# Decoder layer with expert routing: output products of the second attention as three f32r products

## The chip, the cores and the metric

The kernel runs on 1 core of one Trainium2 chip. The metric is the device time of one execution in microseconds; the median of the runs counts. The engines are named as in the profile: PE is TensorE (PEld its weight loads), ACT ScalarE, DVE VectorE, POOL GpSimd, SP SyncE, which only issues DMAs here.

## What is computed

`x` is 32 sequences of 64 tokens of width 256, `ctx_512` 32 x 64 x 64. Three residual parts follow each other:

```python
x = x + attn(layernorm(x), ...)            # 16 heads of 16, rotary, per-head layernorm, softmax
x = x + xattn(layernorm(x), ctx_512, ...)  # below
x = x + ffn(layernorm(x), ...)             # 8 experts, each token to its best 2, weighted

# xattn: 16 heads, keys and values are the context itself (64 wide, rotated: kv_r)
q_hk = (hidden_q @ Wq.T).reshape(B, S, H, K)
q_big = rope(einsum('bshk,hkq->bshq', q_hk, w_kc_q))
q_r = einsum('bshq,hqr->bhsr', q_big, W_qr)
k_r = einsum('bld,hdr->bhlr', kv_r, W_kr)
attn = softmax(einsum('bhsr,bhlr->bhsl', q_r, k_r))
ctx_c = einsum('bhsl,bld->bhsd', attn, kv_r)
ctx_lat = einsum('bhsd,hkd->bhsk', ctx_c, w_kc_kv)
return ctx_lat.transpose(0, 2, 1, 3).reshape(B, S, H*K) @ Wo.T
```

The kernel folds `w_kc_kv` into `Wo` once: the contexts `ctx_c` (16 heads x 64 = 1024 values of a token) are multiplied with one folded 1024 x 256 matrix. These are the output products that the change is about.

## The kernel before

All is one program with an order written out by hand for each engine, and semaphores between them.

**First attention (about 0 to 200 us).** The 32 sequences go in 8 chunks of 4. Each engine walks a list sorted by the times in the tables `AT` and `ONCE` (`in_order`): these numbers set only the order. Between the chunks stand pieces of preparation for later stages. Two of them matter here. `outputs_T` transposes `Wo` on PE and copies it by ACT to `woT`; `outputs_fold` (four times, g = 0 to 3) multiplies it with `w_kc_kv` into bank 4, and ACT copies that to `wop`, 8 blocks of 128 x 256 (lines 688 and 1728). On POOL the list has the square roots of the first norm ("pow") and the addition of the output bias to x for each chunk ("xb", line 1907).

**Second attention (about 210 to 541 us).** The sequences go in 4 blocks of 8 (`blk`). A block has a rope stage (12 tiles n of `half_products`, which are three f32r products with high and low parts, `mm3`, line 397) and then steps s = 0 to 12. In step s the engines do for different sequences b:

- PE: `cross_weights_T` for b = s-3 (transposes of the normalised exponentials `ex` into bank 6), `cross_scores` for b = s, `contexts` for b = s-4 (into bank 7, for b over 2 also bank 1), up to step 4 a tile of the next block's `half_products`, and from step 6 on half an output tile, `cross_out(blk, t, part)`: 4 of the 8 products of a tile of 128 tokens. The fourth tile of a block is done whole in the next block's rope stage at n = 6. `contexts(blk, b)` waits until context b-1 has been read from its bank (`c_cn`).
- ACT: `cross_weights_T` copies bank 6 to `ssb` (line 1794), `cross_exp` makes 8 exponentials of 128 x 64 (line 1785). In block 3, steps 7 to 10 each also round one expert's weights to f32r (`weights_high`, 128 x 1536).
- DVE: row maxima for the exponentials, the reciprocal of their sum, `context_out` for b = s-4, which copies the context from PSUM to `qc` (line 1485), the addition of an output tile to x, and in block 3 the low parts of the expert weights (`weights_low`, line 1504), each after its `weights_high`.
- POOL: the exponentials times the reciprocal, the rope sums, the indirect DMAs of the routing.

`qc` holds first the latent queries of the block and is overwritten, sequence by sequence, with the contexts.

**Experts (from 541 us).** 39 tiles of 128 gathered rows, each with f32r products in high and low parts; no product of it is touched.

## Time and profile before

| | us |
|---|---|
| Median of 3 runs (670.31 to 672.01) | 671.04 |
| The profiled execution | 671.66 |
| its span, first to last instruction | 669.8 |
| PE busy | 599.4 (89%) |
| DVE busy | 494.1 (74%) |
| ACT busy | 336.5 (50%) |
| POOL busy | 251.2 (37%) |

The profile is of one execution. Times within it are microseconds from the start of its span. A row of the order in time gives start, duration, engine, line, operation, what it writes and reads, and its count; a bracket says how long the engine had been idle and for whom it waited. An engine can take the next instruction a little before the end that the record gives, so the distance of two starts, not the duration, is what an instruction costs in a full queue. Matmul ends are modelled. The granted clock of PE is given as a share of 2.4 GHz: 1.00, or 0.50 for 1.2 GHz. A busy share is a mean over stages; the rows further down are read stage by stage.

### The profile page before, as it was taken

Reading aid. Unit: us, or ns where it says so; the run is one execution under the profiler, and the core shown is the slowest. Engines: PE = TensorE matmul, PEld = TensorE weight load, DVE = VectorE, ACT = ScalarE, POOL = GpSimd, SP = SyncE. Lnnn points to the kernel's source line nnn. Section 1 sums busy time; section 2 is a strip of 40 time slices with the busy share of each in tenths; the row PEclk is TensorE's granted clock in tenths of the full one; section 3 lists DMA queues with packets and bytes.
Section 4 is the critical chain, followed back from the end, with each engine's and each line's share of the span. In section 5 each row is a group of like instructions: output and inputs, shape, how many; then the busy total and the mean of one; then the engine's idle time right before and its main releaser. Section 6 shows DMA issues by size and latency. Waiting matters only on the chain.

```text
span 669.8 us, 14896 instructions
## 1 busy us (share of the span) xinstructions
PE 599.4 (89%) x5522; PEld 454.1 (68%) x5522; DVE 494.1 (74%) x1173; ACT 336.5 (50%) x1175; POOL 251.2 (37%) x228
## 2 busy tenths in 40 slices
PE   2787989998899999999999999999987889799990
PEld 1556777777778766776777766777655578688880
DVE  4899799998366797737987389874885876555567
ACT  1377999999572024741157212670336844355550
POOL 2104000000003853833457834766445513643432
PEclk9897999998799999999999999999997999799996
DMA  8699990000000000000000120002036113333376
GB/s 288 174 337 342 325 319 8 2 2 1 1 2 17 17 0 3 2 1 17 1 2 2 64 64 1 2 9 94 12 107 210 49 48 95 113 110 110 98 258 212
DMA packets 40583, 58.96 MB, mean 88 GB/s; under 512 B 14944, under 2 KB 35040, under 8 KB 39872
## 3 DMA queue, kind: packets, MB, share of 16 engines
q1 hardware_dynamic: 34096, 45.94, 22.3%
q0 software_dynamic: 3408, 9.34, 3.8%
q10 hardware_dynamic: 3008, 2.72, 1.3%
q8 instruction: 45, 0.74, 0.5%
q14 instruction: 26, 0.21, 0.1%
HBM read 46.56 MB, written 29.40 MB: 113 GB/s over the span
## 4 chain that ended last, share of the span: by engine, by line
PE 67%; DVE 16%; ACT 9%; issue 5%; DMA 1%; another core or an unknown queue 1%; ACTq 0%; DVEq 0%
PE bank L395 58%; PE bank L404 9%; ACT ex L1675 2%; DVE x L1574 2%; ACT kbd L1665 2%; DVE nmax L1082 1%; DMA lncol<-in_L_attn_ln_kv_b 1%; DVE wlo L1507 1%; DVE m L1181 1%; ACT ex L1785 1%; DVE yr L1044 1%; DVE hvar L1049 1%; DVE newton L1065 1%; ACT xth L1631 1%
## 5 line engine op out<-in xcount | busy, mean ns | idle before, releaser
L1946 POOL TENSOR_TENSOR r<-m,m 128x512 f32<-128x512 f32 x80 | 104.4, 1328 | 102.1 <-DVE m L1181 87.7
L1181 DVE TENSOR_TENSOR m<-bank,cst 128x512 f32<-128x512 f32 x192 | 121.8, 683 | 24.5 <-PE bank L395 20.1
L1785 ACT ACTIVATE ex<-bank,nmax 128x64 f32<-128x64 f32 x256 | 73.1, 337 | 24.3 <-DVE nmax L1473 24.3
L395 PE MATMUL bank<-xth,wbh 128*128 128x512 f32 x192 | 79.9, 416 | 0.0
L395 PE MATMUL bank<-xth,wbl 128*128 128x512 f32 x192 | 75.2, 392 | 0.0
L395 PE MATMUL bank<-xtl,wbh 128*128 128x512 f32 x192 | 75.0, 390 | 0.0
L1768 ACT ACTIVATE qc<-bank 128x512 f32<-128x512 f32 x32 | 17.4, 595 | 101.8 <-PE bank L395 101.8
L395 PE MATMUL bank<-wop,qc 128*128 128x256 f32 x256 | 62.1, 388 | 0.0
L1993 POOL DMA_INDIRECT results<-ys,place x39 | 37.6, 965 | 62.2 <-ACT ys L1857 57.9
L395 PEld LDWEIGHTS bank<-wop,qc 128*128 128x128 f32 x256 | 46.4, 190 | 13.6 <-issue 7.2
L1675 ACT ACTIVATE ex<-bank,nmax 128x64 f32<-128x64 f32 x256 | 54.3, 357 | 2.5 <-DVE nmax L1082 2.4
L1785 ACT ACTIVATION_READ_ACCUMULATOR ex<-bank,nmax 128x1 f32 x216 | 48.9, 227 | 0.0
L404 PE MATMUL bank<-cst,ex 128*128 128x128 f32 x256 | 42.4, 291 | 7.1 <-ACT ex L1675 4.1
L1965 POOL TENSOR_TENSOR ex<-ex,inv 128x512 f32<-128x512 f32 x32 | 33.4, 1042 | 41.0 <-DVE inv L1483 40.7
L1911 POOL TENSOR_TENSOR x<-x,borow 128x512 f32<-128x512 f32 x8 | 10.2, 1286 | 100.5 <-DVE xhat L1014 76.1
L395 PEld LDWEIGHTS bank<-xth,wbh 128*128 128x128 f32 x192 | 36.0, 188 | 16.5 <-issue 8.1
L395 PE MATMUL bank<-r,wqk 64*64 64x512 f32 (+1 forms) x512 | 46.2, 601 | 0.2 <-DVE r L1191 0.2
L404 PEld LDWEIGHTS bank<-cst,ex 128*128 128x128 f32 x256 | 30.7, 147 | 20.3 <-issue 6.9
L395 PEld LDWEIGHTS bank<-xth,wbl 128*128 128x128 f32 x192 | 36.0, 188 | 8.1
L395 PEld LDWEIGHTS bank<-xtl,wbh 128*128 128x128 f32 x192 | 36.1, 188 | 6.4
L1959 POOL DMA_INDIRECT slots<-mxhat,index x32 | 32.8, 1026 | 9.7 <-issue 8.7
L1847 ACT ACTIVATE sg<-bank 128x256 f32<-128x256 f32 x39 | 15.0, 383 | 41.8 <-issue 23.8
(241 smaller groups left out, 1426.9 us busy)
## 6 DMA issues: line engine op xcount, KB each, us to landing
slots<-in_fill SPq DMA_DIRECT2D x1, 17544.0 KB, 65.3
xs<-slots SPq DMA_DIRECT2D x39, 129.0 KB
gb<-results SPq DMA_DIRECT2D x6, 512.0 KB, 4.7
wo_s<-in_L_xattn_Wo SPq DMA_DIRECT2D x1, 2048.0 KB, 18.1
wq_s<-in_L_xattn_Wq SPq DMA_DIRECT2D x1, 2048.0 KB, 11.8
wraw<-in_L_ffn_Wg SPq DMA_DIRECT2D x8, 256.0 KB, 3.8
wraw<-in_L_ffn_Wu SPq DMA_DIRECT2D x8, 256.0 KB, 4.1
wraw<-in_L_ffn_Wd SPq DMA_DIRECT2D x8, 256.0 KB, 4.8
```

The source lines that it names most:

```text
L395: return e.matmul(o, l, r, start=start, stop=stop, skip_group_check=True)
L404: last = e.transpose(o, i, ident)
L1181: last = e.tensor_tensor(m4[n % 2][m][:, :].rearrange("p (b s) -> p b s", s=S), products[half][:, :].rearrange("p (b s) -> p b s", s=S), t ...
L1574: e.scalar_tensor_tensor(tile(t), gb[n][:, m, k, :], share[:, t, k:k + 1], tile(t), ALU.mult, ALU.add).then_inc(t_comb, 1)
L1675: last = e.activation(ex[u][:, h * 64:(h + 1) * 64], bank[3 + u % 2][:, h * 64:(h + 1) * 64], ACT.Exp, bias=nmax[u][:, h:h + 1], scale=1.0)
L1768: e.activation(qc[:, 2 * g + pair, :], latent_banks(blk, g)[pair][:, :], ACT.Copy).then_inc(c_qb, 1)
L1785: last = e.activation(ex[b % 4][:, h * 64:(h + 1) * 64], score_banks(b)[odd][:, n * 64:(n + 1) * 64], ACT.Exp, bias=nmax[b % 4][:, 4 * odd ...
L1847: e.activation(sg[i % 2][:, :], bank[1 + i % 2][:, 0:F], ACT.Silu).then_inc(t_silu, 1)
L1946: last = e.tensor_tensor(rope[n % 6][half][:, :], m4[n % 2][first][:, :], m4[n % 2][second][:, :], op)
L1959: e.indirect_dma_start(out=slots[:, :], out_offset=bass.IndirectOffsetOnAxis(ap=index[:, 4 * b + t, k:k + 1], axis=0), in_=mxhat[:, t, :], ...
L1965: e.tensor_tensor(segments(ex[b % 4]), segments(ex[b % 4]), per_head(inv[b % 2]), ALU.mult).then_inc(c_exn, 1)
L1993: e.indirect_dma_start(out=results[:, :], out_offset=bass.IndirectOffsetOnAxis(ap=place[:, i:i + 1], axis=0), in_=ys[i % YS][:, :], in_off ...
```

## The change

The output products of the second attention are no longer one f32 product each but three f32r products (`mm3`): high part of the context with high part of the folded weights, high with low, and low with high. For this

- ACT copies each folded block twice, raw to `wop_raw` and rounded to `wop` (f32r), and POOL makes the low part `wopl` = raw - high in place of the raw copy (`outputs_low`, four times, "wpl" in the list of POOL's order);
- in the steps, ACT writes the high part of each context to `qch` (`context_high`, over `qc`), and DVE, which used to copy, subtracts it from the same bank to get the low part (`context_out`); DVE waits for ACT (`c_ch`), PE for DVE as before (`c_cn`). The low parts lie in the block's own `xth`/`xtl`, whose content is used up by then (`qcl`);
- buffers move to make room: `mxT` over `ssb`, the routing tables and `woT` over `ex`, `an` and `aT` over `wkv_s`, some of the gathered-row buffers; the early routing tables get buffers of their own;
- ACT's rounding of expert weights also waits for the output products of the third block (`c_co`, 12).

The core of the diff:

```diff
-                w.wait_ge(c_ctxv, i + 1)
-                if b > 2:
-                    for part in range(2):
-                        last = e.tensor_copy(qc[:, 4 * part:4 * part + 4, b * 64:(b + 1) * 64],
-                                             context_banks(b)[part][:, 256 * part:256 * part + 256].rearrange("p (n s) -> p n s", s=S))
-                    last.then_inc(c_cn, 1)
-                else:
-                    e.tensor_copy(qc[:, :, b * 64:(b + 1) * 64], bank[7][:, :].rearrange("p (n s) -> p n s", s=S)).then_inc(c_cn, 1)
+                w.wait_ge(c_ch, i + 1)
+                for heads_of, values_of in context_parts(b):
+                    last = e.tensor_tensor(qcl(blk, b // 2)[:, heads_of, 64 * (b % 2):64 * (b % 2) + 64], values_of,
+                                           qch[:, heads_of, b * 64:(b + 1) * 64].bitcast(F32), ALU.subtract)
+                last.then_inc(c_cn, 1)
...
+            def context_high(blk, b):
+                i = 8 * blk + b
+                w.wait_ge(c_ctxv, i + 1)
+                for heads_of, values_of in context_parts(b):
+                    last = e.activation(qch[:, heads_of, b * 64:(b + 1) * 64], values_of, ACT.Copy)
+                last.then_inc(c_ch, 1)
...
                 for s in range(13):
+                    if 4 <= s < 7:
+                        context_high(blk, s - 4)
                     if 3 <= s < 11:
                         cross_weights_T(blk, s - 3)
+                    if 7 <= s < 12:
+                        context_high(blk, s - 4)
                     if s < 8:
                         cross_exp(blk, s)
...
+                w.wait_ge(s_wpl, 4)
                 for n in range(4 * NP // 8 * part, 4 * NP // 8 * (part + 1)):
-                    last = mm(e, out_bank(blk, t)[:, 0:D], qc[:, n, t * P:(t + 1) * P], wop[:, n, :], n == 0, n == NP - 1)
+                    last = mm3(e, out_bank(blk, t)[:, 0:D], qch[:, n, t * P:(t + 1) * P], qcl(blk, t)[:, n, :], wop[:, n, :], wopl[:, n, :],
+                               n == 0, n == NP - 1)
...
-                e.activation(wop[:, 2 * g:2 * g + 2, :], bank[4][:, :].rearrange("p (q n) -> p q n", q=2), ACT.Copy).then_inc(s_wp, 1)
+                src = bank[4][:, :].rearrange("p (q n) -> p q n", q=2)
+                e.activation(wop_raw[:, 2 * g:2 * g + 2, :], src, ACT.Copy)
+                e.activation(wop[:, 2 * g:2 * g + 2, :], src, ACT.Copy).then_inc(s_wp, 1)
...
+            def outputs_low(g):
+                rows = slice(2 * g, 2 * g + 2)
+                w.wait_ge(s_wp, g + 1)
+                e.tensor_tensor(wopl[:, rows, :], wop_raw[:, rows, :], wop[:, rows, :].bitcast(F32), ALU.subtract).then_inc(s_wpl, 1)
...
                 w.wait_ge(c_proj, 72 if n < 2 else 96)
+                w.wait_ge(c_co, 12)
```

**ACT in the steps 6 to 8 of a block, before.** `ssb` rows are the copies of the transposed weights, `ex` rows the exponentials of one sequence (first, and seven more).

```order
L1794 ACTIVATE ssb_64<-bank 128x512 [waits c_ctxv,exT]
L1785 ACTIVATE ex_67,csum_59<-bank,nmax_57 128x64 [waits c_inv,nmax]
L1785 ACTIVATE ex_67,csum_59<-bank,nmax_57 128x64 x7
L1794 ACTIVATE ssb_63<-bank 128x512 [waits c_ctxv,exT]
L1785 ACTIVATE ex_68,csum_60<-bank,nmax_58 128x64 [waits c_inv,nmax]
L1785 ACTIVATE ex_68,csum_60<-bank,nmax_58 128x64 x7
L1794 ACTIVATE ssb_64<-bank 128x512 [waits c_ctxv,exT]
L1794 ACTIVATE ssb_63<-bank 128x512 [waits c_ctxv,exT]
```

The same place after; `qch` is the high part of a context.

```order
L1809 ACTIVATE qch<-bank 128x8x64 [waits c_ctxv]
L1816 ACTIVATE ssb_64<-bank 128x512 [waits exT]
L1800 ACTIVATE ex_68,csum_59<-bank,nmax_57 128x64 [waits c_inv,nmax]
L1800 ACTIVATE ex_68,csum_59<-bank,nmax_57 128x64 x7
L1816 ACTIVATE ssb_63<-bank 128x512 [waits exT]
L1809 ACTIVATE qch<-bank 128x4x64 [waits c_ctxv]
L1809 ACTIVATE qch<-bank 128x4x64
L1800 ACTIVATE ex_69,csum_60<-bank,nmax_58 128x64 [waits c_inv,nmax]
L1800 ACTIVATE ex_69,csum_60<-bank,nmax_58 128x64 x7
L1816 ACTIVATE ssb_64<-bank 128x512 [waits exT]
L1809 ACTIVATE qch<-bank 128x4x64 [waits c_ctxv]
L1809 ACTIVATE qch<-bank 128x4x64
```

A high part now stands in each step, in front of the copy in step 6, between the copy and the exponentials in step 7, and between two copies after that.

**POOL at the start, before.** `x<-x,borow` is the bias addition of a chunk, `rstds` the square roots of a group of the norm.

```order
L1905 TENSOR_TENSOR rstds<-tops,cst 128x2x2 [waits top]
L1905 TENSOR_TENSOR rstds<-tops,cst 128x2x6 [waits top]
L1911 TENSOR_TENSOR x<-x,borow 128x512 [waits xhat,borow_made]
L1905 TENSOR_TENSOR rstds<-tops,cst 128x2x8 [waits top]
L1911 TENSOR_TENSOR x<-x,borow 128x512 [waits xhat] x7
```

The same place after.

```order
L1932 TENSOR_TENSOR rstds<-tops,cst 128x2x6 [waits top]
L1938 TENSOR_TENSOR x<-x,borow 128x512 [waits xhat,borow_made]
L1947 TENSOR_TENSOR wopl<-wop_raw,wop 128x512 [waits out_fold]
L1932 TENSOR_TENSOR rstds<-tops,cst 128x2x8 [waits top]
L1947 TENSOR_TENSOR wopl<-wop_raw,wop 128x512 [waits out_fold] x2
L1938 TENSOR_TENSOR x<-x,borow 128x512 [waits xhat]
L1947 TENSOR_TENSOR wopl<-wop_raw,wop 128x512 [waits out_fold]
L1938 TENSOR_TENSOR x<-x,borow 128x512 [waits xhat] x6
```

Four subtractions come in behind the first bias addition, around the last square roots and the second addition.

## Rows read from the trace of the kernel before

**Rows 1.** Chain that ended last: shares of the span by engine (page)

```profile
PE 67%; DVE 16%; ACT 9%; issue 5%; DMA 1%; another core or an unknown queue 1%; ACTq 0%; DVEq 0%
```

**Rows 2.** Busy us of each engine by stage: PE, PEld, DVE, ACT, POOL; PEclk, DMA share, GB/s

```profile
340.00:381.00 41.00, 40.68 (x465) 30.52 (x456) 27.76 (x61) 23.81 (x136) 30.85 (x28) 1.00 0.07 24
497.00:541.00 44.00, 33.88 (x430) 24.73 (x422) 32.89 (x84) 30.06 (x106) 17.68 (x16) 0.92 0.45 143
```

**Rows 3.** Order in time, PE, block 1: start us, us, instruction, count

```profile
363.91 1.89 PE L395 MATMUL bank<-wop,qc 128*128 128x256 f32 x8
365.64 0.60 PE L404 MATMUL bank<-cst,ex 128*128 128x128 f32 x4
...
369.59 0.66 PE L395 MATMUL bank<-ssb,kvr 64*64 64x256 f32 x8
...
372.54 0.66 PE L395 MATMUL bank<-ssb,kvr 64*64 64x256 f32 x8
...
383.35 3.69 PE L395 MATMUL bank<-wop,qc 128*128 128x256 f32 x16
386.97 1.95 PE L395 MATMUL bank<-r,wqk 64*64 64x512 f32 x16
```

**Rows 4.** Order in time, PE, value projection of the first attention

```profile
100.07 0.36 PE L395 MATMUL bank<-w1h,xth 128*128 128x256 f32 x1
...
101.58 0.49 PE L647 MATMUL bank<-cst,wqr_s 96*64 96x96 f32 x4
```

**Rows 5.** Order in time, ACT, block 1

```profile
364.16 0.64 ACT L1794 ACTIVATE ssb<-bank 128x512 f32<-128x512 f32 x1
...
366.95 0.70 ACT L1794 ACTIVATE ssb<-bank 128x512 f32<-128x512 f32 x1
367.66 0.31 ACT L1785 ACTIVATE ex<-bank,nmax 128x64 f32<-128x64 f32 x1
...
369.99 0.63 ACT L1794 ACTIVATE ssb<-bank 128x512 f32<-128x512 f32 x1
```

**Rows 6.** Order in time, DVE, block 1

```profile
370.32 0.76 DVE L1490 COPY qc<-bank 128x256 f32<-128x256 f32 x2 [1.93 <-PE bank L395]
370.99 0.41 DVE L1502 TENSOR_TENSOR x<-bank,x 128x256 f32<-128x256 f32 x1
```

**Rows 7.** Order in time, ACT, block 3

```profile
527.38 0.63 ACT L1794 ACTIVATE ssb<-bank 128x512 f32<-128x512 f32 x1
```

**Rows 8.** Order in time, DVE, block 3

```profile
526.30 0.70 DVE L1490 COPY qc<-bank 128x256 f32<-128x256 f32 x2
...
527.55 2.46 DVE L1507 TENSOR_TENSOR wlo<-wraw,whi 128x1536 fp32r<-128x1536 f32 x1 [0.22 <-issue]
...
530.60 1.74 DVE L1507 TENSOR_TENSOR wlo<-wraw,whi 128x1536 fp32r<-128x1536 f32 x1
```

**Rows 9.** Order in time, ACT, near the start

```profile
33.66 0.60 ACT L1730 ACTIVATE wop<-bank 128x512 f32<-128x512 f32 x1
34.15 0.59 ACT L1726 ACTIVATE woT<-bank 128x512 f32<-128x512 f32 x1
```

**Rows 10.** Order in time, POOL, near the start

```profile
55.80 2.56 POOL L1911 TENSOR_TENSOR x<-x,borow 128x512 f32<-128x512 f32 x2
```

**Rows 11.** Order in time, DVE, near the start (in brackets: idle before, releaser)

```profile
55.79 0.22 DVE L1063 TENSOR_TENSOR newton<-hstd 128x64 f32<-128x64 f32 x1
56.04 1.17 DVE L1065 TENSOR_TENSOR newton<-newton,half_v 128x64 f32<-128x64 f32 x1
...
69.96 0.69 DVE L1022 TENSOR_TENSOR xtl<-bank,xth 128x512 fp32r<-128x512 f32 x1 [3.38 <-ACT xth L1631]
```

**Rows 12.** Order in time, PE: two pauses; between them a stretch's clock by windows

```profile
162.25 1.98 PE L395 MATMUL bank<-wkrT,wqrT 64*64 64x64 f32 x32 [1.82 <-ACT wkrT L1699]
...
164.00:168.00 4.00, 4.00 (x50) 0.50 0.00 0
...
528.15 0.63 PE L404 MATMUL bank<-cst,ex 128*128 128x128 f32 x4 [1.14 <-ACT ssb L1794]
```

More of the change, by code:

```diff
@@ L171, in decoder @@
         inv = [keep(f"inv{i}", [P, 8]) for i in range(2)]
+        ssb_at = keep.at
         ssb = [keep(f"ssb{i}", [P, 512]) for i in range(2)]
+        mxT = Space(nc, ssb_at)("mxT", [P, KD, 512])
+        ex_at = keep.at
         ex = [keep(f"ex{i}", [P, 512]) for i in range(4)]
+        tables = Space(nc, ex_at)
+        past, pastgap, pastnext = (tables(n, [P, TILES[1], 2 * E]) for n in ("past", "pastgap", "pastnext"))
+        upto = tables("upto", [P, 2 * E, 2 * E])
+        assert tables.at <= keep.at
         split_at = keep.at
@@ L249, in decoder @@
         mxhat = s4("mxhat", [P, 4, D + 2])
-        mxT_at = s4.at
-        tables = Space(nc, mxT_at)
-        mxT = s4("mxT", [P, KD, 512])
-        past, pastgap = tables("past", [P, TILES[1], 2 * E]), tables("pastgap", [P, TILES[1], 2 * E])
-        upto = tables("upto", [P, 2 * E, 2 * E])
-        assert tables.at <= s4.at
         full = s4("full", [P, E, CAP // P])
@@ L275, in decoder @@
         a2 = Space(nc, max(s1.at, kept.at))
-        wop = a2("wop", [P, NP, D])
+        wop = a2("wop", [P, NP, D], F32R)
+        low_at = a2.at
+        wopl = a2("wopl", [P, NP, D], F32R)
+        wop_raw = Space(nc, low_at)("wop_raw", [P, NP, D])
         s2 = Space(nc, a2.at)
+        qch = Space(nc, a2.at)("qch", [P, NP, 512], F32R)
         qc = a2("qc", [P, NP, 512])
@@ L310, in decoder @@
         ys = [s7(f"ys{i}", [P, D]) for i in range(YS)]
-        pairs = [s7(f"gb{i}", [P, 2, 2, D]) for i in range(5)]
+        pairs = [s7(f"gb{i}", [P, 2, 2, D]) for i in range(6)]
+        ones = [s7(f"gb{i}", [P, 1, 2, D]) for i in range(6, 8)]
         assert s7.at <= after_scores
-        pairs.append(Space(nc, mxhat_at)("gb5", [P, 2, 2, D]))
-        s8 = Space(nc, low.at)
-        ones = [s8(f"gb{i}", [P, 1, 2, D]) for i in range(6, 9)]
-        ones.append(Space(nc, mxT_at)("gb9", [P, 1, 2, D]))
+        s8 = Space(nc, mxhat_at)
+        ones += [s8(f"gb{i}", [P, 1, 2, D]) for i in range(8, 10)]
         gb = pairs + ones
@@ L425, in decoder, with context_parts @@
         OUT_AT = {6: 0, 8: 1, 10: 2}
+        qcl = lambda blk, t: (xths, xtls)[t % 2][blk % 2][:, :, :].rearrange("p k (m s) -> p (k m) s", s=P)
+        def context_parts(b):
+            if b > 2:
+                return [(slice(4 * part, 4 * part + 4), context_banks(b)[part][:, 256 * part:256 * part + 256].rearrange("p (n s) -> p n s", s=S))
+                        for part in range(2)]
+            return [(slice(0, NP), bank[7][:, :].rearrange("p (n s) -> p n s", s=S))]
         pos_bank = lambda b: bank[1] if b < 3 else bank[7]
@@ L1333, in route_count, with upto_of, past_of @@
                 e.tensor_tensor(full[:, :, :], count.broadcast_to([P, E, n]), in_tiles(C("fill")[:, 0:n], E), ALU.is_gt).then_inc(r_route, 1)
-            def upto_of(counts, n):
+            def upto_of(to, counts, n):
                 le = C("le").rearrange("p (i j) -> p i j", j=2 * E)
-                e.tensor_tensor(upto[:, 0:n, 0:n], le[:, 0:n, 0:n], in_tiles(counts, n), ALU.mult).then_inc(r_tab, 1)
-            def past_of(n, entries):
+                e.tensor_tensor(to[:, :, :], le[:, 0:n, 0:n], in_tiles(counts, n), ALU.mult).then_inc(r_tab, 1)
+            def past_of(to, n, entries):
                 number = C("iota")[:, 0:n].rearrange("p (n o) -> p n o", o=1).broadcast_to([P, n, entries])
-                e.tensor_tensor(past[:, 0:n, 0:entries], number, in_tiles(ends[:, 0:entries], n), ALU.is_ge).then_inc(r_tab, 1)
+                e.tensor_tensor(to[:, :, :], number, in_tiles(ends[:, 0:entries], n), ALU.is_ge).then_inc(r_tab, 1)
             def early_table():
@@ L1361, in early_table @@
                 e.tensor_scalar(own[:, 0:n], C("iota")[:, 0:n], float(P), C("part"), ALU.mult, ALU.add)
-                e.tensor_reduce(expert[:, 0:n], past[:, 0:n, 0:E], AX, ALU.add)
-                e.tensor_tensor(pastgap[:, 0:n, 0:E], past[:, 0:n, 0:E], in_tiles(gap[:, 0:E], n), ALU.mult).then_inc(r_tab, 1)
+                e.tensor_reduce(expert[:, 0:n], early_past[:, :, :], AX, ALU.add)
+                e.tensor_tensor(early_gap[:, :, :], early_past[:, :, :], in_tiles(gap[:, 0:E], n), ALU.mult).then_inc(r_tab, 1)
                 w.wait_ge(r_tab, 5)
@@ L1921, in gpsimd @@
                     add_bias(c)
+                elif name == "wpl":
+                    outputs_low(c)
                 else:
```

26 lines of the change are left out of this document (14 added, 12 removed).

## Prediction

> **What bounds the kernel now.** I read the chain that ended last first, then the busy time by stage, then the order in time of each engine where the edit touches it. In the chain [rows 1] the reader should see that two thirds of the span is TensorE's (PE), so time taken off a product can count. The stage table says where. In the second attention of block 1 (the second block of 8 sequences; block 0 and block 2 run alike) PE is busy 40.68 of 41 us at the full granted clock; in the same stage of block 3 it is busy 33.88 of 44 us [rows 2]. So a saving on PE is paid out in blocks 0 to 2 and not in block 3. The order in time shows, last, how thin the cover of the other engines is where the output products lie: in block 1 ScalarE (ACT) runs from the copy at 364.16 to the one at 369.99 with hardly a gap [rows 5], and these are the steps into which the change puts more work for it.
>
> I count steps as the code does: s is a step of the second attention, and sequence b is scored at step b, and its context is made at step b+4. Half an output tile (4 of 8 products) stands on PE in each of the steps 6 to 11, and the fourth tile whole in the next block's rope stage.
>
> **The products.** Before, half a tile is four f32 products, each in two instructions: it begins at 363.91 and the next work at 365.64, 1.73 us [rows 3]. After, it is twelve f32r products of 128x256. The trace has just that: the value projection issues twelve f32r products of 128x256, each with its own 128x128 weights, from 100.07 to the next f32 work at 101.58, 1.51 us [rows 4]. Gain 0.22 to 0.23 us for a half. The fourth tile, 16 instructions between f32r products, takes 383.35 to 386.97, 3.62 us [rows 3]; 24 at 1.51/12 = 0.126 us and less at the joints (its neighbour in front is f32r already) make 2.9, gain 0.7. A block has six halves and one whole tile: 6 x 0.23 + 0.7 = 2.1 us, four blocks 8.3 us. That is the ceiling on PE.
>
> The rows give 1.73/4 = 0.43 us for an f32 product and 3 x 0.126 = 0.38 for its three f32r ones. The Trainium skill, FP8 and Floating Point Precision, TensorE Precision Notes, says that true FP32 takes four passes through the array. With three passes of the same length in their place a half would gain a quarter, 0.43 us, and the three blocks would give 5 us more; the rows show half of that, and they are used.
>
> **What is added in the steps of blocks 0 to 2.** DVE's copy of the context out of PSUM becomes two things in a row: ACT writes the high part, then DVE subtracts. DVE's part costs what it did: two copies of 128x256 take 0.76 us, and a tensor_tensor of 128x256 with one PSUM input takes 0.41, two of them 0.33 + 0.42 = 0.75 [rows 6]. ACT's part is new: 32 of them, 20 us in all. A 128x512 PSUM copy on ACT holds the engine 0.49 us when more is queued, and ends 0.60 after its start (33.66, and the next copy at 34.15 [rows 9]); for sequences 3 to 7 it is two pieces of 256, which I take as 0.54 us to hold the engine and 0.65 to finish.
>
> For b = 0 and 1 it falls into idle time of ACT and costs nothing. Then ACT has no gap. The high parts of b = 2 (0.49) and b = 3 (0.54) come before the weights' copy that now starts at 369.99 [rows 5]. Of this 0.22 fits into a wait for the row maximum (366.95 to 367.66 is 0.71, a copy needs 0.49), so that copy starts at 369.99 + 1.03 - 0.22 = 370.80. Behind it the high part of b = 4 starts 0.49 later and ends 0.65 after that, 371.94; DVE's subtraction ends at 372.71, and PE may start context 5, which waits for that bank to be read, at about 372.75. Before it started at 372.54 [rows 3], and by its own work PE would now be there at about 372.1 (three halves of 0.23 less 0.24 of small waits). So the first three halves' gain is lost and 0.2 more. Context 6 and 7 find their waits met within 0.05 us: from one context to the next PE takes 2.95 us (369.59 to 372.54 [rows 3]), now 2.7, and the new chain (context end, 0.65 ACT, 0.75 DVE, 0.1 of hand-over) 1.5 to 2. What is left for a block: -0.2 + two halves 0.46 + the half of step 11 0.23 + the whole tile 0.7 = 1.2 us. **Three blocks: -3.6 us.** Bounds: if ACT is in nobody's way -6.2; if the chain is 0.3 us longer than I make it, it binds at contexts 5, 6 and 7, and a block keeps only 0.2 to 0.3, so -0.8. I take the middle since each number has a row close by.
>
> **Block 3.** Up to step 7 DVE sets the pace (it makes the early table there), and the high parts fall into ACT's idle time. Then ACT runs the last exponentials, the rounding of one expert's weights and the copy at 527.38 [rows 7], and only behind these the high part of b = 4: 527.38 + 0.49 + 0.65 = 528.5. DVE did its copy for b = 4 at 526.30 and went on to the low parts of the expert weights at 527.55 [rows 8]. Now its subtraction waits until 528.5, and the low parts start at 528.52 + 0.75 + 0.33 = 529.6, 2.0 us later. From there to the start of the experts DVE worked without a gap, so nearly all of it is passed on; 0.5 comes back because the first of these took 2.46 us beside GpSimd work against 1.74 for the next [rows 8]. **+1.5 us**, bounds +0.5 (ACT's row is ahead of where I put it) and +2.5. PE's own gain of this block is hidden: it was idle a quarter of the time.
>
> **The start.** The folded output weights are now copied twice by ACT, raw and high, four times. Between 33.66 and 34.15 [rows 9] one such copy holds ACT 0.49 us, and it stands on the chain: the transposed Wo copy behind it is what PE waits for. The first is passed on whole; of the other three two fall into gaps of ACT, and one I take for 0.3. About +0.8.
>
> GpSimd (POOL) gets four subtractions of 128x512. They are needed only 200 us later, but they are queued between its others: the square roots and the second bias addition wait behind them, and both have over 10 us to spare. What counts is whom they block. The trace shows two bias additions of POOL from 55.80 to 58.36 [rows 10], and in that time a 128x64 step of DVE takes 1.17 us, where the like one in front of it took 0.22 [rows 11], and the step behind it as long: about 0.95 us lost for each POOL operation that meets a DVE instruction with two SBUF inputs. After the change the additions move back by 2.5 to 4 us, which spares those two DVE steps (-1.1 on the chain, the row maxima come sooner), and POOL is busy six operations long while DVE rotates the next chunk, with 4 to 5 us lost where DVE has 3.4 us to spare (its wait before 69.96 [rows 11]). **Start in all +0.5**; bounds -1.5 (the steps are spared and the rest hidden) and +2.5 (four blocked steps of 1 us, of which a part shows, and the copies).
>
> The Trainium skill, SBUF — State Buffer, Who interferes with whom, says that a DVE instruction with two SBUF inputs contends with a GpSimd instruction that reads SBUF, and that one with at most one SBUF input does not. The trace agrees for the first. By that rule the four new POOL operations speak against the change (rival 4), and the new DVE subtractions, with one input in PSUM, do not.
>
> Buffers that move (tables, gathered rows, mxT) change no count of instructions; the tables have their own early copies, and I cost them at nothing. The added wait of the expert rounding for the third block's output products is met some 15 us before.
>
> **Sum.** +0.5 - 3.6 + 1.5 = -1.6 us. On the profiled execution, 671.66 us (span 669.8 and 1.9 around it), 670.1; on the median of the runs, 671.04, **669.4 us**. A measurement of this kernel can tell about 0.3%, 2.0 us, from no change.
>
> **Rivals.**
> 1. *ACT's part is hidden.* The chain in the steps is met in time, a block gives 1.9 to 2.1, the start costs nothing: -6.0 + 0 + 1.0 = -5, 666.0 us. For it: PE waits a third of a microsecond in these steps today without harm. Against: ACT's row is full from 364 to 370 [rows 5]. 20%.
> 2. *ACT's part binds from context 4 on.* Each context waits for ACT and DVE, a block gives 0.2 to 0.3: -0.8 + 0.5 + 2.0 = +1.7, 672.7 us. For it: my slack at contexts 6 and 7 is only 0.05 to 0.5 us. 15%.
> 3. *Slower: the granted clock.* A pause of 1.82 us before 162.25 is followed by a stretch at half clock, 1.2 GHz [rows 12]. In block 3 PE's pause before the transposes at 528.15 grows from 1.14 us [rows 12] to about 1.4, and two more of 0.4 to 0.6 follow. If the clock falls there, the last contexts and output tiles, 6 to 7 us of PE work, take twice that, and about 4 us show before the experts start: -1.6 + 4 = +2.4, 673.4 us. It decides if the clock is lost between 526 and 532. Against: the 1.14 us cost no clock. 8%.
> 4. *Slower: POOL's subtractions block DVE on the chain.* Four times 0.95, and no step spared in return: the start costs 0.8 + 3.8 = 4.6, so 4.6 - 3.6 + 1.5 = +2.5, 673.5 us. For it: the price is there [rows 10, 11]. Against: the row after, where DVE waits 3.4 us for ACT [rows 11]. It decides if DVE's wait there is gone. 8%.
> 5. *The products gain nothing*, since the joints take it all: 0.5 + 1.5 = +2, 673.0 us. Against: the ladder of f32r products [rows 4]. 2%.
>
> **How the numbers follow.** Forecast case 47%, 667.8 to 671.4 by its own bounds. Faster by over 0.3% (below 669.0): rival 1 and somewhat over four tenths of the forecast case, 0.40. Slower by over 0.3% (above 673.1): six tenths of rivals 3 and 4, a third of rival 2, half of rival 5, 0.16. The rest, 0.44, is within 0.3%. The range goes from 666.3 to 673.2: it leaves a tenth on either side.
>
> **What the profile after would show.** Each half tile 1.5 us from its first product to the next work and the whole tile 2.9; if not, the first term is wrong. In block 1, a PE wait of about 0.6 us before context 5 put down to DVE's subtraction, and none at 6 and 7; waits at all three mean rival 2, none means rival 1. Block 1 from its first half_products to those of block 2 shorter by 1.2 us. In block 3, DVE idle some 2 us before the subtraction for b = 4, by ACT. At the start, DVE steps of 128x64 at 0.22 us where they took 1.2, and others later that are longer. A granted clock below 1.00 between 526 and 540 means rival 3. The forecast fails outright if the start shifts by more than 3 us either way, since none of its rows show the new mix of POOL and DVE.

## The result, and the profile after

The changed kernel takes **673.67 us** (median of 20 runs, 670.03 to 675.95) against 671.0 for the kernel before in the same series. The ratio is 1.0045, with a 95% interval of 1.0033 to 1.0057: **slower by 3.0 us** by the ratio (the two medians differ by 2.7), where 1.6 us less was forecast. The profiled execution takes 673.4 us (span 671.4), against 671.66 (span 669.8) before.

TensorE does have less to do. The page of the changed kernel, its first part (busy us, share of the span, instructions) and the first line of its chain, which answers to [rows 1]:

```profile
PE 591.9 (88%) x5650; PEld 454.4 (68%) x5650; DVE 495.4 (74%) x1173; ACT 356.4 (53%) x1231; POOL 256.1 (38%) x232
...
PE 61%; DVE 15%; ACT 13%; issue 5%; DMA 2%; another core or an unknown queue 1%; ACTq 0%; POOL 0%; SPq 0%; DVEq 0%; POOLq 0%
```

PE is busy 7.5 us less than before (599.4), ACT 19.9 us more, and PE's share of the chain fell from 67% to 61% while ACT's rose from 9% to 13%. The work was taken away, and other engines were waited for instead.

ACT copies the transposed context once in each block, at the same point of the program. Its starts are milestones. Changed kernel, one answer for each block (line, engine, tile, count: shortest, median and longest ns, first and last start in us):

```profile
L1788 ACT ACTIVATE kvT<-bank x1: 600/600/600, 240.4 to 240.4; 128x512 f32<-128x512 f32 x1
L1788 ACT ACTIVATE kvT<-bank x1: 597/597/597, 317.2 to 317.2; 128x512 f32<-128x512 f32 x1
L1788 ACT ACTIVATE kvT<-bank x1: 598/598/598, 398.8 to 398.8; 128x512 f32<-128x512 f32 x1
L1788 ACT ACTIVATE kvT<-bank x1: 597/597/597, 479.0 to 479.0; 128x512 f32<-128x512 f32 x1
```

Before, they stand at 241.4, 319.3, 399.8 and 480.1. The three distances are 76.8, 81.6 and 80.2 now, and were 77.9, 80.5 and 80.3. The first (the second attention of block 0 and the rotation of block 1) is 1.1 us shorter, as forecast. The next is 1.1 us **longer**, the third 0.1 shorter: in all 0.1 us gained where 3.6 were due.

The steps themselves went as forecast. Order in time on PE in block 1 of the changed kernel: contexts 4 to 7 and the start of the whole fourth tile (start us, us, instruction; in brackets the idle time ahead and who ended it).

```profile
367.41 0.66 PE L401 MATMUL bank<-ssb,kvr 64*64 64x256 f32 x8
...
370.81 0.66 PE L401 MATMUL bank<-ssb,kvr 64*64 64x256 f32 x8 [0.62 <-DVE xth L1505]
...
373.45 0.66 PE L401 MATMUL bank<-ssb,kvr 64*64 64x256 f32 x8
...
375.77 0.66 PE L401 MATMUL bank<-ssb,kvr 64*64 64x256 f32 x8
...
383.01 0.36 PE L401 MATMUL bank<-wop,qch 128*128 128x256 f32 x1 [2.19 <-DVE x L1515]
```

Context 5 waits 0.62 us for DVE's subtraction, 6 and 7 don't wait. Context 7 comes at 375.77, which was 378.01 before: 2.2 us earlier. And then the last row: ahead of the whole fourth tile PE stands still for 2.19 us, and all of it is gone. In block 2 the same row has 0.81 us. Before, there was no wait there ([rows 3], 383.35).

What PE waits for is a bank. The third tile's products are in bank 0, DVE adds them to x, and the fourth tile goes into the same bank. DVE in block 1 of the changed kernel:

```profile
378.13 0.75 DVE L1505 TENSOR_TENSOR xtl<-bank,qch 128x256 fp32r<-128x256 f32 x2 [2.18 <-ACT qch L1809]
382.44 0.42 DVE L1515 TENSOR_TENSOR x<-bank,x 128x256 f32<-128x256 f32 x1 [3.55 <-remote]
```

PE's last product of that tile, and in the kernel before the last half tile, and DVE's addition behind it:

```profile
377.78 0.28 PE L401 MATMUL bank<-wop,xth 128*128 128x256 f32 x1
```

```profile
378.60 1.99 PE L395 MATMUL bank<-wop,qc 128*128 128x256 f32 x8
```

```profile
382.78 0.42 DVE L1502 TENSOR_TENSOR x<-bank,x 128x256 f32<-128x256 f32 x1 [2.10 <-remote]
```

"Remote" means that the profile finds no instruction that ended when the wait did. The addition waits for one semaphore only, PE's. Before, PE ended at 380.59 and the addition began at 382.78, 2.2 us later. Now PE ends at 378.06 and the addition begins at 382.44, 4.4 us later. **PE's signal arrives late, and at nearly the same time as before, however early the work was done.** (Matmul ends are modelled, but in e9 below the same two rows are 0.04 us apart, so the model does not make these 4 us.) Before, the addition ended at 383.20 and PE wanted the bank at 383.35: the lateness was covered, with 0.15 us to spare. Now PE wants it at 380.8.

It is not DVE that is held. ACT waits for PE too, for context 7, which ends at 376.43 (375.77 + 0.66):

```profile
377.44 0.66 ACT L1809 ACTIVATE qch<-bank 128x256 fp32r<-128x256 f32 x2 [2.60 <-PE bank L401]
```

ACT begins 1.0 us after that end, and in e9 0.06 us after it. ACT's own signal is not late: ACT ends at 378.10 and DVE's subtraction begins at 378.13. And PE takes up DVE's signal in 0.15 us (382.86, 383.01). What is late is what PE sends.

POOL tells what goes on at that time. Changed kernel, POOL in block 1, the last of eight scatters of normalized tokens to memory, and what follows:

```profile
372.48 1.01 POOL L1993 DMA_INDIRECT slots<-mxhat,index  x1 [0.16 <-issue]
...
380.11 0.96 POOL L1993 DMA_INDIRECT slots<-mxhat,index  x1 [0.30 <-issue]
381.10 1.10 POOL L1965 TENSOR_TENSOR kvr<-ctxs,cst 128x512 f32<-128x512 f32 x1
```

The last seven scatters run one behind the other, 1.27 us apart. Block 0 has none, and block 0 kept its gain. The late release keeps its distance from this row and not from PE's work: it comes 2.33 us after the last scatter's start (380.11, 382.44), and before 2.34 (380.44, 382.78). In block 2 of the changed kernel DVE waits twice, first for the third tile and then for the next block's first product:

```profile
462.68 0.42 DVE L1515 TENSOR_TENSOR x<-bank,x 128x256 f32<-128x256 f32 x1 [2.82 <-remote]
464.21 2.48 DVE L1197 TENSOR_TENSOR m<-bank,cst 128x512 f32<-128x512 f32 x4 [1.10 <-remote]
```

POOL's last scatter there:

```profile
461.75 0.96 POOL L1993 DMA_INDIRECT slots<-mxhat,index  x1 [0.30 <-issue]
```

The first wait ends 0.93 us behind the last scatter's start, so PE lost only 0.81 us there, and the second 2.46. In blocks 1 and 2 of this trace, of the kernel before and of e1, e2, e3 and e12 the last late release lies 2.3 to 2.5 us behind the start of the row's last scatter, twelve times out of twelve.

**Block 3** runs from its kvT copy to DVE's last addition at 542.94: 63.9 us, 61.3 before. ACT and DVE there:

```profile
524.95 1.52 ACT L1829 ACTIVATE whi<-wraw 128x1536 fp32r<-128x1536 f32 x1
526.33 0.63 ACT L1816 ACTIVATE ssb<-bank 128x512 f32<-128x512 f32 x1
526.80 0.70 ACT L1809 ACTIVATE qch<-bank 128x256 fp32r<-128x256 f32 x2
```

```profile
527.53 0.76 DVE L1505 TENSOR_TENSOR xth<-bank,qch 128x256 fp32r<-128x256 f32 x2 [2.20 <-ACT qch L1809]
...
533.94 0.76 DVE L1505 TENSOR_TENSOR xtl<-bank,qch 128x256 fp32r<-128x256 f32 x2 [1.33 <-ACT qch L1809]
```

DVE waits for the high part of sequence 4, as forecast, behind the expert weights' rounding and the weights' copy. The stretch of block 3 that follows, from the stage table (us; busy PE, PEld, DVE, ACT, POOL; PEclk), has the granted clock at 0.57, where before it was 1.00:

```profile
529.00:533.00 4.00, 4.00 (x26) 3.34 (x24) 3.62 (x4) 2.81 (x5) 0.00 (x0) 0.57 0.21 68
```

### The profile page after: what moved, and what is told of

Same layout as the page of the kernel before. It is cut to its first block, busy times and chain, and to the rows that moved or that the text cites. A ratio compares the mean times of both kernels' runs of the same rounds, so it can differ in the third digit from the quotient of the medians.

```text
span 671.4 us, 15183 instructions
## 1 busy us (share of the span) xinstructions
PE 591.9 (88%) x5650; PEld 454.4 (68%) x5650; DVE 495.4 (74%) x1173; ACT 356.4 (53%) x1231; POOL 256.1 (38%) x232
## 4 chain that ended last, share of the span: by engine, by line
PE 61%; DVE 15%; ACT 13%; issue 5%; DMA 2%; another core or an unknown queue 1%; ACTq 0%; POOL 0%; SPq 0%; DVEq 0%; POOLq 0%
PE bank L401 53%; PE bank L410 8%; ACT ex L1800 4%; ACT ex L1688 2%; DVE nmax L1098 2%; ACT kbd L1678 1%; DMA lncol<-in_L_attn_ln_kv_b 1%; DVE wlo L1520 1%; ACT qch L1809 1%; DVE m L1197 1%; DVE yr L1060 1%; DVE hvar L1065 1%; ACT ssb L1816 1%; DMA gb<-results 1%
## 5 line engine op out<-in xcount | busy, mean ns | idle before, releaser
L1800 ACT ACTIVATION_READ_ACCUMULATOR ex<-bank,nmax 128x1 f32 x216 | 51.4, 248 | 0.0
L401 PE MATMUL bank<-wop,qch 128*128 128x256 f32 x128 | 39.1, 305 | 3.1 <-DVE x L1515 2.2
L401 PE MATMUL bank<-ssb,kvr 64*64 64x256 f32 x256 | 29.7, 408 | 9.7 <-DVE xth L1505 5.7
L401 PE MATMUL bank<-whi,txh 128*128 x78 | 35.4, 453 | 1.2 <-DVE wlo L1520 1.2
```

The source lines that it names most:

```text
L401: return e.matmul(o, l, r, start=start, stop=stop, skip_group_check=True)
L1800: last = e.activation(ex[b % 4][:, h * 64:(h + 1) * 64], score_banks(b)[odd][:, n * 64:(n + 1) * 64], ACT.Exp, bias=nmax[b % 4][:, 4 * odd ...
```

## The experiments

The runs were made on several chips, and these turned out to be of two kinds. Kernels of one series ran on one chip, beside the kernel before, so ratios are compared, and us only within a kind. On the first kind (the result, e1 to e4, e12, e13) the kernel before takes 670.5 to 671.0 us, and every trace has waits of DVE and ACT marked "remote"; on the second (e5 to e11) it takes 662.8 to 663.5, and no trace has one anywhere. The traces of the first kind show the late signals above in blocks 1 and 2, but for e4 and e13, which move the scatters: they have none there. Every experiment's chip was met in one series only, so these runs can't tell a property of the chip from one of its state at that time. "Kind" is meant so below.

On the first kind, in every kernel, DVE also waits 3.55 to 3.58 us for PE before one row maximum of block 3 (518.23 in the kernel before), where on the second it waits at most 2.4. This may be why block 3 is longer there whatever the kernel; it is not shown.

All milestones in one table (us from one kvT copy to the next, and from the last to DVE's last addition; "kind" says whether the chip showed late signals anywhere). The unedited kernel before has a trace on the first kind alone; on the second e5 stands in for it:

| kernel | kind: late signals | block 0 | block 1 | block 2 | block 3 | ratio to before (95%) |
|---|---|---|---|---|---|---|
| before | yes | 77.9 | 80.5 | 80.3 | 61.3 | 1 |
| changed | yes | 76.8 | 81.6 | 80.2 | 63.9 | 1.0045 (1.0033-1.0057) |
| e1 start alone | yes | 77.9 | 80.4 | 80.4 | 61.2 | 1.0016 (0.9996-1.0036) |
| e12 the same | yes | 77.8 | 80.5 | 80.4 | 61.5 | 1.0014 (0.9999-1.0030) |
| e2 block 3 in f32 | yes | 76.8 | 80.9 | 80.2 | 66.1 | 1.0088 (1.0056-1.0119) |
| e3 block 3 alone | yes | 77.9 | 80.4 | 80.5 | 62.6 | 1.0031 (1.0016-1.0046) |
| e4 scatters split | yes | 76.8 | 79.1 | 79.2 | 62.6 | 0.9965 (0.9945-0.9986) |
| e13 and ACT's order | yes | 76.8 | 79.2 | 79.2 | 62.0 | 0.9975 (0.9953-0.9997) |
| e5 before, split | no | 77.8 | 80.3 | 80.2 | 59.5 | 1.0000 (0.9981-1.0018) |
| e9 changed | no | 76.8 | 79.1 | 79.2 | 62.5 | 0.9989 (0.9972-1.0006) |
| e10 scatters split | no | 76.8 | 79.2 | 79.2 | 60.7 | 0.9999 (0.9981-1.0017) |
| e11 block 3 alone | no | 77.9 | 80.2 | 80.3 | 60.9 | 1.0036 (1.0018-1.0054) |
| e6 split, ACT's order | no | 76.8 | 79.1 | 79.2 | 60.6 | 0.9976 (0.9961-0.9990) |
| e7 split, block 3 f32 | no | 76.8 | 79.2 | 79.1 | 59.4 | 0.9989 (0.9967-1.0010) |
| e8 scatters later | no | 76.8 | 79.2 | 81.6 | 62.5 | 1.0041 (1.0014-1.0069) |

**e1 and e12, the start alone.** All blocks go back to one f32 product:

```
+        OLD = (0, 1, 2, 3)
...
+                    if blk in OLD:
+                        last = mm(e, out_bank(blk, t)[:, 0:D], qc[:, n, t * P:(t + 1) * P], wop[:, n, :].bitcast(F32), n == 0, n == NP - 1)
+                        continue
...
+                    for heads_of, values_of in context_parts(b):
+                        last = e.tensor_copy(qc[:, heads_of, b * 64:(b + 1) * 64], values_of)
```

> The start of the changed kernel (raw copy, high part, subtraction on POOL) with the second attention as before: DVE copies the context, one f32 product in all four blocks. The product reads the high part of the weights alone, so the low part of the weights is missing from the result. Theory A (from the two traces: between 40 and 66 us the changed kernel goes from 1.0 us ahead to 0.6 us behind, and what it wins later is TensorE's clock): the start costs 1.0 to 1.6 us, 672.0 to 672.6 us. Rival B (the prediction's +0.5 with its bounds, or a start that is hidden): 670.5 to 671.5 us.

> The start of the changed kernel with the second attention as before in all four blocks (the product reads the high part of the weights alone), once more: its first interval, 0.9996 to 1.0036, leaves the prediction's +0.5 us and the trace's +1.6 us both open. Theory A: 1.0010 to 1.0020 with or without late signals. Rival B: 1.0000 to 1.0008.

Measured: 1.0016 and 1.0014, so about +1.0 us; the two intervals together leave 0 to 2 us open (the medians alone differ by 0.2 and 0.8). The prediction's +0.5 is inside, and so is all of theory A: the two are not told apart. The profiles don't help, since the start of a single execution varies by more: with the changed kernel's start the first kvT copy stands anywhere from 237.9 to 241.8 us on this kind. Below, the sum of the parts takes 1.0, and it could be 1 us more or less by that.

**e2, block 3 in one f32 product,** `OLD = (3,)`, and POOL adds the high and low weights together before it:

```
+                    if blk == 3 and s == 0:
+                        w.wait_ge(c_co, 12)
+                        e.tensor_tensor(wop_raw[:, :, :], wop[:, :, :].bitcast(F32), wopl[:, :, :].bitcast(F32), ALU.add).then_inc(s_sum, 1)
```

> Changed kernel with block 3 as before (DVE copies, one f32 product; POOL adds high and low weights back together once, in the 9.7 us in which it is idle before its first normalization of block 3). Theory A: block 3 costs 2.6 us (span between the last keys' transpose copy and the last residual addition 61.3 before, 63.9 after), all of it DVE waiting for ACT's high part and the clock; without it 673.7 - 2.6 = 671.1 us. Rival C: block 3 is not the cause, the blocks 0 to 2 are: 673.5 us.

Both theories missed: 675.5 us, and block 3 takes 66.1 us. The trace has the reason, POOL first, then DVE and PE:

```profile
489.07 4.53 POOL L2030 TENSOR_TENSOR wop_raw<-wop,wopl 128x2048 f32<-128x2048 f32 x1
```

```profile
490.40 4.35 DVE L1213 TENSOR_TENSOR r<-m,m 128x512 f32<-128x512 f32 x2
```

```profile
494.80 3.56 PE L402 MATMUL bank<-r,wqk 64*64 64x512 f32 x16 [3.23 <-DVE r L1213]
```

DVE's two rotation sums, with both inputs in SBUF (the core's working memory), take 4.35 us beside POOL's addition; in the changed kernel they take 1.29 (492.74), with POOL idle. POOL's idle time was not free. So e2 priced my own edit, and not block 3.

**e3, block 3 alone,** `OLD = (0, 1, 2)`.

> Changed kernel with blocks 0 to 2 as before and the three products in block 3 alone (in blocks 0 to 2 the f32 product reads the high part of the weights alone; the low part is missing there). Theory A: blocks 0 to 2 gain almost nothing in the changed kernel (0.1 us in its trace), so this is as slow as the changed kernel: 673.5 to 674.5 us. Rival D: the blocks do gain the forecast 3.6 us and block 3 loses more than the trace says: 677 us.

1.0031, the changed kernel 1.0045: taking the three blocks' products back costs nothing, if anything it gains. Rival D (677 us) is out, and theory A's 673.5 to 674.5 was missed too, on the other side: 672.4 us. Block 3 is 1.3 us longer than before (62.6 to 61.3), with the clock at full from 513.4 us to the end of the block.

**e4, the scatters split.**

```
-            SCATTER_AT = [{7: (0,), 8: (1,), 9: (2, 3), 10: (4, 5), 11: (6, 7)}] * 3 + [{3: (0,), 4: (1,), 5: (2, 3), 6: (4,), 7: (5, 6), 8: (7,)}]
+            SCATTER_AT = [{7: (0,), 8: (1,), 9: (2,), 10: (3,), 12: (4, 5, 6, 7)}] * 3 + [{3: (0,), 4: (1,), 5: (2, 3), 6: (4,), 7: (5, 6), 8: (7,)}]
...
+                    if blk < 3 and s == 12:
+                        context(blk + 1)
                     if blk and s in SCATTER_AT[blk]:
                         for n in SCATTER_AT[blk][s]:
                             scatter(blk - 1, n)
-                    if blk < 3 and s == 12:
-                        context(blk + 1)
```

> Changed kernel; in blocks 1 and 2 POOL issues the first four scatters one per step (steps 7 to 10) and the other four after the position product of the context, behind the last output product of the third tile. Theory A: TensorE's signals reach DVE late while scatters run back to back (1.0 to 4.4 us late in the trace), DVE adds the third tile late, and TensorE waits 2.2 and 0.8 us for bank 0 before the whole fourth tile. With the scatters behind it these waits go: 2 to 3.5 us less than the changed kernel, 670.2 to 671.7 us. Rival E: the wait is DVE's own or the lateness moves with the scatters onto the rotation products of the next block: within 0.5 us of the changed kernel, 673.2 to 674.2 us.

668.28 us, 0.9965: by the ratios 5.4 us less than the changed kernel (3.8 to 7.0 by the two intervals), from the order of POOL's queue alone, and more than theory A's 2 to 3.5. Blocks 0, 1 and 2 are now shorter than before by 1.1, 1.4 and 1.1 us: 3.6. DVE adds the third tile in block 1 at

```profile
375.63 0.41 DVE L1515 TENSOR_TENSOR x<-bank,x 128x256 f32<-128x256 f32 x1
```

with no wait, and PE has none ahead of the fourth tile. Of the measured gain 2.5 + 1.0 us stand in blocks 1 and 2; block 3 lost no clock among its last tiles in this execution, 1.3 us more; the rest is within the intervals. The edit also makes POOL's product for the next context earlier. That this is the gain, and not the signals, is ruled out by e5 and e10 below: where no signal is late the same edit gains nothing.

**e5, the same split in the kernel before.**

> The kernel before with the scatters of blocks 1 and 2 split as in the run on the changed kernel (four in steps 7 to 10, four after the context's position product). Theory A (the changed kernel's gain in blocks 0 to 2 was swallowed by a DVE addition whose release does not move; the kernel before covers the same lateness with its own products, since TensorE waits 0 us ahead of its whole fourth tile there): it gains little, 0 to 1 us, 669.5 to 670.5 us. Rival F (the split helps either kernel alike, and says nothing of the change): 5 us less, 665.5 us.

1.0000: the split alone is worth nothing to the kernel before. But this series had the kernel before at 662.8 us, and its trace shows no late signal in blocks 1 and 2, so it does not exclude rival F where they are late. There the trace of the kernel before speaks against F: PE had no wait that the split could take away.

**e8, all scatters behind the context's product:** the edit of e4 with `{12: range(8)}` for blocks 1 and 2, on the second kind of chip.

> Changed kernel with all eight scatters of blocks 1 and 2 behind the context's position product, in one run of about 10 us. Theory A (TensorE's signals come late once about five scatters have run back to back): the lateness moves onto the rotation products of the next block, TensorE's or DVE's waits of 1 to 3 us stand there instead, and half or more of the gain of the split is lost: 670 to 673 us. Rival I (only the place at the third tile's addition matters, since nothing else waits for TensorE so closely): as the split, 668.3 us.

1.0041: rival I's number (that of the split) is out, and the loss is the one that theory A foresaw, but not by its mechanism: eight scatters run back to back from 380.76 to 390.84, and no signal of PE is late beside them. What the shift did is push POOL's rotation sum onto DVE's own:

```profile
390.87 2.52 POOL L1980 TENSOR_TENSOR r<-m,m 128x512 f32<-128x512 f32 x2
```

```profile
390.76 3.78 DVE L1207 TENSOR_TENSOR r<-m,m 128x512 f32<-128x512 f32 x2 [0.76 <-PE bank L401]
```

3.78 us instead of 1.29; PE then waits 0.43 us at 405.89, the clock is at half from 406.5 for 3.4 us, and block 2 is 2.4 us longer. "So many scatters in a row make signals late" is wrong as a rule for any chip; on the first kind this order was not run. The two kinds had to be told apart.

**e9 to e11: the changed kernel, the split and block 3 alone once more.**

> The changed kernel unaltered, once more, since the two sets of runs so far differ: in the first (before 670.5 us) TensorE's signals reach DVE and ACT up to 4 us late while scatters run, in the second (before 662.8 us) none does, though scatters run. Ratio to the kernel before. Theory A: the loss hangs on the late signals; where the trace shows them, 1.0045; where it shows none, TensorE has no wait ahead of the whole fourth tiles, the blocks 0 to 2 keep their 3.6 us and the ratio is 0.997 to 0.999. Rival J: the ratio is 1.0045 with or without late signals.

> Changed kernel with the scatters of blocks 1 and 2 split, once more. Theory A: 0.9965 where signals are late; where none is late, the same as the changed kernel unaltered, within 0.1% (0.997 to 0.999 of before). Rival J: 0.8% faster than the changed kernel in either case.

> Changed kernel with blocks 0 to 2 as before (the f32 product there reads the high part of the weights alone; the low part is missing) and three products in block 3 alone, once more. Theory A: start and block 3 cost the same in either case, 1.003 of before; where no signal is late, 0.5% above the changed kernel, since the three blocks' gain of 3.6 us is what it lacks. Rival J: within 0.1% of the changed kernel.

This series met a chip without late signals, and theory A holds in e9 and e11 to the number, in e10 in the main (0.9999, where 0.997 to 0.999 was written). The changed kernel, unaltered, is at 0.9989, 0.7 us faster than before, with an interval that reaches 1.0006: no slower, and not surely faster. The split adds nothing (0.9999, their intervals overlap widely); without the three blocks' products it is at 1.0036, so these are worth 0.47%, 3.1 us, and by the traces 3.2 (235.1 us for three blocks against 238.3 in e5). DVE and PE in e9 (the last products of the third tile, and the milestones):

```profile
376.80 0.76 DVE L1505 TENSOR_TENSOR xtl<-bank,qch 128x256 fp32r<-128x256 f32 x2 [1.23 <-ACT qch L1809]
377.70 0.42 DVE L1515 TENSOR_TENSOR x<-bank,x 128x256 f32<-128x256 f32 x1
```

```profile
377.26 0.28 PE L401 MATMUL bank<-wopl,qch 128*128 128x256 f32 x1
377.38 0.28 PE L401 MATMUL bank<-wop,xth 128*128 128x256 f32 x1
```

```profile
L1788 ACT ACTIVATE kvT<-bank x1: 598/598/598, 316.8 to 316.8; 128x512 f32<-128x512 f32 x1
L1788 ACT ACTIVATE kvT<-bank x1: 599/599/599, 395.9 to 395.9; 128x512 f32<-128x512 f32 x1
L1788 ACT ACTIVATE kvT<-bank x1: 598/598/598, 475.1 to 475.1; 128x512 f32<-128x512 f32 x1
```

The last product ends at 377.66, the addition begins at 377.70: 0.04 us, where it was 4.4. POOL's scatters run in e9 as in the first trace, at 372.09, 373.40, 374.67 and on to 379.72, 1.27 apart. Rival J (the same ratios with or without late signals) is out.

**e6 and e13, the split and ACT's order in block 3:** each of the last four roundings of expert weights one step later, behind the high part.

```
-                    if blk == 3 and 7 <= s < 11:
-                        weights_high(s - 5)
+                    if blk == 3 and 8 <= s < 12:
+                        weights_high(s - 6)
```

> Changed kernel with the scatters split, and in block 3 ACT makes the high part of context 4 ahead of the expert weights' high part (each of the last four weights one step later). Theory A: DVE's wait of 2.2 us for the high part of context 4 and with it 1 to 1.5 us of block 3 goes: 667 us against 668.3 us of the split alone. Rival G: DVE waits as long for the weights' high part instead, 668.3 us or more.

> Changed kernel with the scatters split and ACT's order in block 3 changed, once more: is it faster than the kernel before in both surroundings? Theory A: 0.9965 or less where signals are late, 0.9976 again where none is. Rival G: 0.999 or more, its first ratio was chance.

DVE's wait for the high part of sequence 4 falls from 2.20 to 0.83 us (its subtraction at 520.98 in e6), but it then waits 0.28 for the rounding, and block 3 is 60.6 us against 60.7: the gain is not passed on in this trace. In the other kind of chip it is 62.0 against 62.6. The kernel is at 0.9976 and 0.9975, **faster than the kernel before on both kinds**, by 1.6 us; so rival G's 0.999 is out, but theory A's 0.9965 or less on the first kind was not reached. What of it is due to ACT's order can't be told from e4 (0.9965) and e10 (0.9999).

**e7, the split and block 3 in f32,** with POOL's sum in two halves, at 472.54 and 494.70, where DVE does no rotation sum.

> Changed kernel with the scatters split, and block 3 with one f32 product of the weights' high and low parts added up by POOL in two halves, one after DVE has normalized the tokens of block 2 and one after DVE's first maximum of block 3 (the earlier run made the sum at once beside DVE's rotation sum, which took 4.35 us for two where it takes 1.29). Theory A: the half sums delay DVE by under 0.5 us, and block 3 is 1.3 us shorter than in three products and loses no clock: 666.5 to 667.5 us. Rival H: POOL's additions delay DVE wherever they stand, each by about its own length of 2.2 us: 669 us or more.

Block 3 takes 59.4 us, that of the kernel before (59.5), so DVE is not delayed and rival H is out: against it three products in block 3 cost 1.3 us (e10) to 3.1 (e9). Yet the ratio is 0.9989, only 0.7 us under the 0.9999 of the split on this kind (theory A had 0.8 to 1.8), and the intervals overlap. The lead of 2.9 us that it has over e9 when the experts start shrinks to 1.0 at one row of PE; e7 and e9:

```profile
582.32 0.44 PE L411 MATMUL bank<-cst,xs 128*128 128x128 f32 x2 [3.03 <-DMA xs<-slots]
```

```profile
583.34 0.44 PE L410 MATMUL bank<-cst,xs 128*128 128x128 f32 x2 [1.13 <-DMA xs<-slots]
```

The load of this gathered tile is held until the last scatters have landed (the DMA queue of SP waits for them, 8.5 us in e7 and 6.6 in e9). POOL begins the last scatter at 574.69 in e7 and at 577.60 in e9, so it keeps the whole lead. The load goes out at 580.15 and 581.22, 5.5 and 3.6 us later. So 1.9 us of the lead are lost between a scatter's issue and its landing; why the landing takes longer in e7 was not found.

## Why the prediction was wrong, point by point

- **The products**: right. From the first product of a half tile at 376.36 to the next work at 377.90 are 1.54 us, in other steps 1.49 to 1.56 (forecast 1.51), and 1.73 in front of context 7, which took 1.92 before; the whole tile takes 2.99 (2.9).
- **The steps of blocks 0 to 2**: right, down to the single waits (0.62 us at context 5, none at 6 and 7). Block 0 gained 1.1 us, and with no late signals or the scatters split all three gain 3.2 to 3.6 in all. Rivals 1 and 2 are out. (One sum in the prediction is off: with a quarter gained on every product the three blocks would give about 4.4 us more by its own numbers, not 5. Nothing hangs on it.)
- **"The whole tile 0.7", and with it -3.6 for three blocks: the step that failed.** It took for granted that PE may begin the whole fourth tile when its own work is done. No term asked when bank 0 is free. The kernel before has the answer in two rows: DVE's addition ends at 383.20, and PE's tile begins at 383.35. An engine that gets there 2.2 us sooner runs into that wait if the addition doesn't move too, and the addition did not hang on PE's pace: its idle time was marked "remote", 2.10 us, in blocks 1 and 2 and not in block 0. PE waited 2.19 us in block 1 and 0.81 in block 2 for the bank, and on chips of this kind the term of -3.6 measured -0.1 us. Taking the late signals away, by the order of the scatters (e4) or by the chip (e9), gives -3.6 and -3.2. On a chip like that of e9 the forecast would have been off by 0.9 us instead of 4.6, and that would have been luck as far as this step goes: it never asked for the bank.
- **Block 3, +1.5**: right in size, 1.3 us in e3 and e4 (62.6 - 61.3), 1.2 in e10 (60.7 - 59.5), 1.4 in e11. DVE's wait for sequence 4 is there; it is 2.20 us long.
- **Rival 3, the granted clock in block 3**, given 8%: it came to pass in the profiled execution, at 529.3 us, just behind PE's pauses of 1.45 and 0.62. The same code in block 3 takes 62.6 us in e4 and 63.9 here; in e9, again with such a stretch (0.58 from 523 to 527), 62.5, and 60.7 in e10 without. So it costs 1.3 to 1.8 us when it comes, under half of the 4 us put on it. (The 1.8 is an upper value: earlier in the block e9 also has two stretches of 6.8 us at half clock where e10 has two of 3.4.) It does not come each time: of seven profiled executions with three products and ACT's old order in block 3 it falls among the last contexts and tiles in three (this one, e8, e9). Over the 20 runs the changed kernel has a granted clock of 0.957 on average, the kernel before 0.961 over the 29 of e1's series.
- **The start, +0.5**: +1.0 measured, within its bounds. The mechanism was right: DVE's 128x64 steps near 56.5 take 0.23 us now where two took 1.17 and 1.19 [rows 11], and four rows of other steps between 53.09 and 64.5 take 4.9 us more in all; DVE's wait of 3.38 us [rows 11] is 1.24. One detail speaks against the prediction's sentence that an instruction with at most one input in SBUF is not held: two TENSOR_SCALAR of 128x32, with one tensor input in SBUF, take 2.50 us at 58.08 beside POOL's subtractions, where they took 0.37.
- **Rival 4** is out (start +4.6), rival 5 too.

The sum on this kind of chip: +1.0 - 0.1 + 1.3 = 2.2, and with the 1.3 of the clock, when it falls, 3.5; measured 3.0 (2.2 to 3.8). Without late signals: +1.0 - 3.2 + 1.2 to 3.0 = -1.0 to +0.8, measured -0.7. The forecast of -1.6 lies 0.6 us past the first end of that.

## What to carry to other kernels

When a change makes one engine earlier, list every buffer that it takes over from another, and look in the trace how long before its use it was handed over: a margin of 0.15 us is a bound, though no wait is shown. An idle time whose releaser is "remote", or that ends long after the work it waits for, need not move with your change. Look for what it does keep its distance from (here the last scatter of a row on POOL), take it as fixed to that, and count what runs into it. Before you trust a gain or a loss of a few tenths of a per cent, measure on more than one chip: here one kernel was clearly slower on one (1.0045) and not slower on another (0.9989). And where a gain of some us disappears, move what is queued around it on the other engines before giving up the change: here four scatters put behind one product made 1.0045 into 0.9965 on a chip with late signals, and changed nothing on one without.

## What the runs showed of the hardware

- **Signals of PE up to 4.4 us late while POOL scatters to memory**, on some chips and not on others, with the same program (4.4 us in the changed kernel, 0.04 in e9, at the same point). The last of them comes 2.3 to 2.5 us after the start of the last scatter of a row. It is also in the tail, where POOL scatters again: two waits of ACT at 576.21 and 583.38 in the changed kernel are "remote", 2.53 and 2.50 us, and e9 has none. From DVE's last addition to the end the changed kernel takes 128.5 us on one kind and 123.0 in e9; that all of this is late signals is not shown. What makes a signal late was not found. It isn't the number of scatters alone, since on the second kind of chip they run in the same row and rhythm (e9), and eight in a row made none late (e8). The Trainium skill, SBUF — State Buffer, Who interferes with whom, says of the engines' access to SBUF that PE waits on no one. The trace agrees as far as it goes: PE's products kept their 1.5 us a half tile beside the scatters. But who waited for PE waited up to 4.4 us here.
- **POOL's idle time has a price on DVE.** Two rotation sums of DVE took 4.35 us beside a POOL addition of 2048 columns (e2) and 3.78 beside POOL's own sums (e8), against 1.29 alone, while four products with one input in PSUM, from 487.89 on beside POOL's sums and then this addition, kept their 2.47 (e2). The same section says that a DVE instruction with two SBUF inputs contends with GpSimd's reads; e2 and e8 agree, and by this rule e2 could have been foreseen; e7, whose POOL additions stand where DVE does no rotation sum, cost DVE nothing that block 3 shows (59.4 us against 59.5).
